# A two-layer Perceiver block: routing the first expert layer's tokens into slots of 48 per expert

## The reference

```python
E, K, H, F = (64, 6, 256, 96)
CAP = 2 * (T * K // E)                      # 48
...
buf = jnp.zeros((E, CAP + 1, H), x.dtype).at[se, slot].set(x[tok])[:, :CAP]
h = jax.nn.silu(jnp.einsum('ech,ehf->ecf', buf, w_gate)) * jnp.einsum('ech,ehf->ecf', buf, w_up)
out = jnp.einsum('ecf,efh->ech', h, w_down)
...
y = _routed_moe(x, topk_w, topk_ids, w_gate, w_up, w_down)
shared = jax.nn.silu(x @ ws_gate) * (x @ ws_up) @ ws_down
```

## Time and profile before

| | |
|---|---|
| median of three runs | 820.96 us (811.13 to 823.92) |
| profiled execution, its own time | 819.23 us |
| its span | 817.5 us |
| mean granted clock of TensorE | 0.884 of 2.4 GHz |
| first expert layer: first instruction, and first of the next stage | 195.06 and 346.29 us |
| TensorE busy, of the span | 680.8 us (83%) |
| VectorE, ScalarE, GpSimd busy | 534.1, 384.9, 314.9 us |

### The profile page before, as it was taken

One profiled execution on the slowest core, in us unless ns is written; L12 is line 12 of the kernel. 1 busy time (PEld: TensorE's weight loads), 2 busy tenths in 40 slices (PEclk: granted clock), 3 DMA queues, 4 the chain that ended last, 5 costly groups with the idle time before them and its releaser, 6 DMA issues. The chain is left out here.

```text
span 817.5 us, 12900 instructions
## 1 busy us (share of the span) xinstructions
PE 680.8 (83%) x4484; PEld 437.6 (54%) x4484; DVE 534.1 (65%) x771; ACT 384.9 (47%) x727; POOL 314.9 (39%) x233
## 2 busy tenths in 40 slices
PE   3735799987899999878998469888898778999997
PEld 1322345445577776556776225555555455666775
DVE  3379799993422222269999599999989963533221
ACT  2214555542122222234555378898989972303221
POOL 0064589891000000013444077787877871000000
PEclk9976999997999999988999666886868966999999
DMA  9637000003043433032443558586686742930000
GB/s 370 246 131 283 1 0 0 0 1 120 20 155 120 169 115 116 0 110 68 127 127 98 156 127 148 128 177 139 135 165 114 175 91 56 423 158 0 0 0 13
DMA packets 94718, 93.68 MB, mean 115 GB/s; under 512 B 69520, under 2 KB 87120, under 8 KB 88272
## 3 DMA queue, kind: packets, MB, share of 16 engines
q1 hardware_dynamic: 82128, 86.78, 36.5%
q10 hardware_dynamic: 12544, 6.29, 2.6%
HBM read 69.66 MB, written 6.62 MB: 93 GB/s over the span
## 5 line engine op out<-in xcount | busy, mean ns | idle before, releaser
L1489 DVE TENSOR_REDUCE d_nmax<-d_psum 128x1 f32<-128x1024 f32 x128 | 152.8, 1212 | 13.9 <-PE d_psum L1611 13.7
L1611 PE MATMUL d_psum<-d_kst,d_qT 96*128 96x512 bf16 x256 | 105.2, 515 | 36.9 <-DMA d_kst<-kT_scratch 23.4
L430 POOL TENSOR_TENSOR b_h<-b_h,b_cb 128x1024 f32<-128x1024 f32 x32 | 84.6, 2645 | 31.4 <-DVE b_h L484 30.9
L1465 POOL TENSOR_SCALAR d_rounded<-w_early,d_lift 128x1024 f16<-128x1024 f32 x64 | 71.8, 1122 | 29.5 <-ACT d_lift L1566 25.1
L1562 ACT ACTIVATE d_e<-d_psum,d_nmax 128x1024 f32<-128x1024 f32 x64 | 71.2, 1116 | 18.1 <-DVE d_nmax L1489 17.7
L484 DVE TENSOR_TENSOR_SCAN b_h<-b_dA,b_psum 128x1024 f32<-128x1024 f32 x32 | 73.0, 2285 | 7.6 <-PE b_psum L588 4.8
L1562 ACT ACTIVATE w_early<-d_psum,d_nmax 128x1024 f32<-128x1024 f32 x64 | 71.4, 1115 | 13.6 <-DVE d_nmax L1489 13.3
L544 ACT ACTIVATE b_dA<-b_dtT,b_A 128x248 f32<-128x248 f32 x128 | 53.7, 491 | 49.3 <-DVE b_h L484 43.4
L841 DVE TENSOR_TENSOR c_prod<-c_silu,c_psum 128x384 f32<-128x384 f32 x32 | 17.7, 554 | 90.1 <-ACT c_silu L884 90.1
L1465 POOL TENSOR_SCALAR d_rounded<-d_e,d_lift 128x1024 f16<-128x1024 f32 x64 | 72.8, 1137 | 9.6 <-ACT d_lift L1566 2.2
L1275 PE MATMUL k_psum<-k_wkv,k_ctxT 128*128 128x256 f32 x256 | 67.4, 395 | 5.4 <-issue 5.4
(11 more groups left out here) (375 smaller groups left out, 1285.3 us busy)
## 6 DMA issues: line engine op xcount, KB each, us to landing
d_kst<-kT_scratch SPq DMA_DIRECT2D x96, 128.0 KB, 2.7
w_early<-in_w SPq DMA_DIRECT2D x8, 1152.0 KB, 5.1
w_late<-in_w SPq DMA_DIRECT2D x8, 1152.0 KB, 5.1
w<-in_w SPq DMA_DIRECT2D x8, 1088.0 KB, 20.5
b_cb<-c_scratch SPq DMA_DIRECT2D x4, 2048.0 KB, 7.2
kT_scratch<-k_kT ACTq DMA_DIRECT2D x16, 384.0 KB, 2.8
a_ctxT<-in_ctxT SPq DMA_DIRECT2D x2, 2048.0 KB, 12.7
a_ctx<-in_ctx SPq DMA_DIRECT2D x2, 2048.0 KB, 21.2
```

Source lines behind the costliest of these rows:

```text
L430: nc.gpsimd.tensor_tensor(hv, hv, cv, ALU.mult).then_inc(hc_ready, 1)
L1465: nc.gpsimd.tensor_scalar(tile_of(r, j), e[j], lift[t][:, f:f + 1], HALF_ULP_ONE, ALU.mult, ALU.add).then_inc(r_ready, 1)
L1489: nc.vector.tensor_reduce(nm[:, t, m:m + 1, f:f + 1], quarter(m, j).unsqueeze(1), AX.X, ALU.max, negate=True).then_inc(nm_ready, 1)
L1611: last = nc.tensor.matmul(quarter(m, j)[:, b * 512:(b + 1) * 512], qT[0:QROWS, m:m + 1, t * P:(t + 1) * P], kst[m % 2][0:QROWS, at:at + 51 ...
```

## The change

The `MOE0` branches leave `moe_stage`, and a new `moe0_stage` takes its place in the list of stages. It gathers the tokens of four experts into 4 x 48 = 192 slots, computes gate, up and down for the slots only, and adds the results back to the tokens:

- `choose` (VectorE) builds the 0/1 matrix `pick` (128 tokens x 4 experts x 48 slots, bf16) for each half of the tokens by comparing the count `r.pos` with the slot number. A token that did not choose the expert has `FAR` added.
- `gather` (TensorE) multiplies `pick` by the normed input, which is split into three bf16 parts whose sum is the float32 value: 12 bf16 matmuls of 192 columns.
- `gate_up`: for each pair of experts and each half of the features, the two experts' gathered tokens stand in the array as 64 columns each (48 and 16 more that are not used), with results in PSUM partitions 0 to 63 and 64 to 127: 8 float32 matmuls of 192 columns.
- `turn` transposes two tiles of `a`; `turn_back` transposes four tiles of `pickw`, which GpSimd made from `pick` and the router's weights.
- `down`: 4 float32 matmuls of 256 columns, again with 64 columns standing. `add_back`: 4 float32 matmuls of 256 columns with `back` (128 columns) standing, accumulated in `acc[t]`.

In round `it`, TensorE gathers group `it`, does gate and up of `it - 1`, the transposes of `it - 2`, down of `it - 3` and the adding of `it - 4`. There are 16 + 4 rounds, written out. A group's weights come in two transfers, 768 and 384 KB. The accumulator bank is first cleared by a float32 matmul of zeros. The six more semaphores in `g["spent"]` are only cleared by GpSimd. ScalarE's remaining functions, `gate` and `keep_aT`, are a silu of 128x192 and a copy of 96x256 a round.

```diff
+GRP = 4
+NGRP = E0 // GRP
+PAIRS = GRP // 2
+SLOTS = GRP * CAP0
+HALF = P // 2
+GU0 = 2 * F0
+WGU0 = KC * GRP * GU0
+WDN0 = GRP * D
...
+def load_experts0(sp, g, d, grp, s):
+
+    sp.dma_start(g["w0"][s][:, 0:WGU0], d["w0gu"][grp]).then_inc(g["w0_in"][s], 16)
+    sp.dma_start(g["w0"][s][0:F0, WGU0:SLOT0], d["w0dn"][grp]).then_inc(g["w0_in"][s], 16)
...
+    nc.vector.tensor_tensor(r.selb[:, :, :], r.rep[:, :, 0:E0], r.ext[:, :, 0:E0], ALU.not_equal).then_inc(sem_sel, 1)
     step(nc.vector.tensor_tensor(r.sel[:, :, :], r.rep[:, :, 0:E0], r.ext[:, :, 0:E0], ALU.not_equal))
-    nc.vector.tensor_copy(r.selb[:, :, :], r.sel[:, :, :]).then_inc(sem_sel, 1)
+    step(nc.vector.tensor_scalar(r.pos[:, :, :], r.sel[:, :, :], -FAR, FAR, ALU.mult, ALU.add))
...
+                for grp in range(4, NGRP):
+                    sp.wait_ge(down_done, grp - 3)
+                    load_experts0(sp, g, d, grp, grp % 4)
...
+                for grp in range(NGRP):
+                    pool.wait_ge(pick_ready, grp + 1)
+                    if grp >= 2:
+                        pool.wait_ge(back_done, grp - 1)
+                    nc.gpsimd.tensor_tensor(pickw[grp % 2][:, :, :, 0:CAP0], pick[grp % 3][:, :, :, :],
+                                            r.w[:, :, grp * GRP:(grp + 1) * GRP].unsqueeze(3).to_broadcast([P, TC, GRP, CAP0]),
+                                            ALU.mult).then_inc(pickw_ready, 1)
...
+                dve.wait_ge(count_done, 1)
+                nc.vector.tensor_tensor(r.pos[:, :, :], r.pos[:, :, :], count_psum, ALU.add).then_inc(pos_ready, 1)
...
+                def choose(grp):
+                    if grp >= 3:
+                        dve.wait_ge(gather_done, grp - 2)
+                        dve.wait_ge(pickw_ready, grp - 2)
+                    for t in range(TC):
+                        last = nc.vector.tensor_tensor(
+                            pick[grp % 3][:, t, :, :], slot[:, :].unsqueeze(1).to_broadcast([P, GRP, CAP0]),
+                            r.pos[:, t, grp * GRP:(grp + 1) * GRP].unsqueeze(2).to_broadcast([P, GRP, CAP0]), ALU.is_equal)
+                    last.then_inc(pick_ready, 1)
+
+                def multiply(grp):
+                    dve.wait_ge(silu_ready, grp + 1)
+                    if grp >= 2:
+                        dve.wait_ge(aT_done, grp - 1)
+                    nc.vector.tensor_tensor(a[grp % 2][:, :, :], silu[grp % 2][:, :, :], gu_psum[:, :, F0:],
+                                            ALU.mult).then_inc(a_ready, 1)
+
+                def keep_back(grp):
+                    dve.wait_ge(back_done, grp + 1)
+                    if grp >= 3:
+                        dve.wait_ge(added, grp - 2)
+                    nc.vector.tensor_copy(back[grp % 3][:, :, :], st_psum).then_inc(back_ready, 1)
+
+                def keep_out(grp):
+                    dve.wait_ge(down_done, grp + 1)
+                    if grp >= 2:
+                        dve.wait_ge(added, grp - 1)
+                    nc.vector.tensor_copy(out[grp % 2][:, :, :], out_psum).then_inc(out_ready, 1)
+
+                choose(0)
+                choose(1)
+                for it in range(NGRP + 4):
+                    if it + 2 < NGRP:
+                        choose(it + 2)
+                    if 1 <= it <= NGRP:
+                        multiply(it - 1)
+                    if 2 <= it <= NGRP + 1:
+                        keep_back(it - 2)
+                    if 3 <= it <= NGRP + 2:
+                        keep_out(it - 3)
+                dve.wait_ge(added, NGRP)
+                step(nc.vector.tensor_tensor(x[:, :, :], x[:, :, :], ps[:, ACC, :].rearrange("p (t c) -> p t c", t=TC), ALU.add))
...
+                act.wait_ge(xnT_done, 1)
+                nc.scalar.activation(xnT[:, :, :], ps[:, OUT, :].rearrange("p (k t) -> p k t", k=KC),
+                                     ACT.Copy).then_inc(xnT_ready, 1)
+                act.wait_ge(xn_ready, 1)
+                nc.scalar.activation(xp[0][:, :, :], xn[:, :, :], ACT.Copy).then_inc(part_ready, 1)
...
+                def keep_gathered(grp):
+                    act.wait_ge(gather_done, grp + 1)
+                    if grp >= 2:
+                        act.wait_ge(gu_done, grp - 1)
+                    nc.scalar.activation(xT[grp % 2][:, :, 0:SLOTS], xt_psum, ACT.Copy).then_inc(xT_ready, 1)
+
+                def gate(grp):
+                    act.wait_ge(gu_done, grp + 1)
+                    if grp >= 2:
+                        act.wait_ge(a_ready, grp - 1)
+                    nc.scalar.activation(silu[grp % 2][:, :, :], gu_psum[:, :, 0:F0], ACT.Silu).then_inc(silu_ready, 1)
...
+                nc.tensor.matmul(ps[:, ACC, :].rearrange("p (a b) -> p a b", a=4), g["zeros"][:, :],
+                                 g["zeros"][:, :].unsqueeze(1).to_broadcast([P, 4, P]), start=True, stop=False,
+                                 skip_group_check=True)
...
+                def gather(grp):
+                    pe.wait_ge(pick_ready, grp + 1)
+                    if grp >= 1:
+                        pe.wait_ge(xT_ready, grp)
+                    for k in range(KC):
+                        for t in range(TC):
+                            for q in range(3):
+                                last = nc.tensor.matmul(xt_psum[:, k, :], xp[q][:, t, k * P:(k + 1) * P],
+                                                        pick[grp % 3][:, t, :, :].rearrange("p e s -> p (e s)"),
+                                                        start=(t == 0 and q == 0), stop=(t == TC - 1 and q == 2))
+                    last.then_inc(gather_done, 1)
+
+                def gate_up(grp):
+                    pe.wait_ge(g["w0_in"][grp % 4], 32 * (grp // 4 + 1))
+                    pe.wait_ge(xT_ready, grp + 1)
+                    if grp >= 1:
+                        pe.wait_ge(a_ready, grp)
+                    w = g["w0"][grp % 4][:, 0:WGU0].rearrange("p (k e f) -> p k e f", k=KC, e=GRP)
+                    for q in range(PAIRS):
+                        for k in range(KC):
+                            for h in range(2):
+                                e = 2 * q + h
+                                last = nc.tensor.matmul(gu_psum[h * HALF:(h + 1) * HALF, q, :],
+                                                        xT[grp % 2][:, k, e * CAP0:e * CAP0 + HALF], w[:, k, e, :],
+                                                        start=(k == 0), stop=(k == KC - 1), skip_group_check=True)
+                    last.then_inc(gu_done, 1)
+
+                def turn(grp):
+                    pe.wait_ge(a_ready, grp + 1)
+                    if grp >= 1:
+                        pe.wait_ge(aT_ready, grp)
+                    else:
+                        pe.wait_ge(shared_aT_ready, 1)
+                    for q in range(PAIRS):
+                        last = nc.tensor.transpose(at_psum[:, q, :], a[grp % 2][:, q, :], ident[:, :])
+                    last.then_inc(aT_done, 1)
+
+                def turn_back(grp):
+                    pe.wait_ge(pickw_ready, grp + 1)
+                    if grp >= 1:
+                        pe.wait_ge(back_ready, grp)
+                    for q in range(PAIRS):
+                        for t in range(TC):
+                            last = nc.tensor.transpose(st_psum[:, q, t * P:(t + 1) * P],
+                                                       pickw[grp % 2][:, t, 2 * q:2 * q + 2, :].rearrange("p e s -> p (e s)"),
+                                                       ident[:, :])
+                    last.then_inc(back_done, 1)
+
+                def down(grp):
+                    pe.wait_ge(aT_ready, grp + 1)
+                    if grp >= 1:
+                        pe.wait_ge(out_ready, grp)
+                    w = g["w0"][grp % 4][0:F0, WGU0:SLOT0].rearrange("p (e c) -> p e c", e=GRP)
+                    for q in range(PAIRS):
+                        for h in range(2):
+                            last = nc.tensor.matmul(out_psum[h * HALF:(h + 1) * HALF, q, :],
+                                                    aT[grp % 2][:, q, h * HALF:(h + 1) * HALF], w[:, 2 * q + h, :],
+                                                    start=True, stop=True, skip_group_check=True)
+                    last.then_inc(down_done, 1)
+
+                def add_back(grp):
+                    pe.wait_ge(back_ready, grp + 1)
+                    pe.wait_ge(out_ready, grp + 1)
+                    for q in range(PAIRS):
+                        for t in range(TC):
+                            last = nc.tensor.matmul(acc[t], back[grp % 3][:, q, t * P:(t + 1) * P], out[grp % 2][:, q, :],
+                                                    start=False, stop=(grp == NGRP - 1 and q == PAIRS - 1),
+                                                    skip_group_check=True)
+                    last.then_inc(added, 1)
+
+                for it in range(NGRP + 4):
+                    if it < NGRP:
```

(15 more changed lines are left out.)

335 lines of the change are left out of this document (232 added, 103 removed).

## The result

The changed kernel takes 782.85 us (median of four runs: 780.54, 780.86, 784.83, 789.67); the kernel before, measured beside it, took 816.17 (four runs, 811.13 to 823.92). The ratio is 0.967, with a 95% interval of 0.962 to 0.972. It is not the quotient of the two medians, since it leaves out runs more than 1.5% above the fastest of their kernel. The forecast was 784, in a range of 776 to 815.

A forecast was written before the change was run, and what follows sets the result against it. TensorE's streaming was taken to bound the expert stage: start 212.6 + 16 rounds x 5.9 + 1.9 + 0.6 = 309.5, next stage at 310.9 against 346.49. So 819.2 - 35.6 = 784 us, range 776 to 815.

The forecast's parts named there:

- The bound: Expert stage: bound by TensorE's streaming, so a change is worth a sum over its matmuls; new round 5.9 us against 8.40.
- The other engines' work a round: Each round of the new stage: VectorE 2.5 us, ScalarE some 1.2, GpSimd 0.9, all under TensorE's 5.9.
- the margin of the weights: Weight transfers of a group: landing takes 5.1 us, read some 8.8 us later; holds down to rounds of about 3.5 us.
- 64 standing at half price: Gate, up and down: about half the 128-standing price, two experts side by side in different output partitions; 784 us, chance 0.70.
- The price of a record: Gate and up: 0.095 us for each of 16 records of 192 columns, with an allowance for weight loads; 1.5 us a round.
- Rival B: Gate, up and down: 64 standing costs as much as 128; rounds of 7.75 us, kernel 813 us, chance 0.14.
- The changes of width: Four switches between 64 and 128 columns standing in each round: 0.15 us for all four.
- rival C: Every change of width waits for the array to run empty: 0.34 us by 64 changes, kernel 803 us, chance 0.05.
- The beginning: Stage start: gather begins at 212.6 against 212.01; lower clock costs 1.9 us, the second gather's wait 0.6.
- The end: Last rounds run down without waits; last matmul ends at 309.5, next stage starts 1.4 us later, at 310.9 against 346.49.
- Rivals D and E: D: stage at 1.2 GHz throughout, kernel 878, chance 0.07. E: hand-over, transfer or fetching paces rounds, 802, chance 0.04.
- everything behind the barrier stays: Stages after the expert stage: move forward unchanged, so the whole 35.6 us saving comes off the profiled 819.2.

The follow-up runs named there:

- the repeat: The changed kernel run once more without an edit: profiled 792.56 us, expert stage 122.0 us, median of six runs 784.97, ratio 0.969 to the kernel before.
- the two repeats: The kernel before and the changed kernel, each profiled once more without an edit: 821.11 and 792.56 us, expert stages 149.8 and 122.0 us.
- the last run: The changed kernel once more, unedited, measured beside three others: median of six runs 784.97 us, ratio 0.969 to the kernel before.

## Why the prediction held, and where it did not

**The bound was right.** The stage is a sum of TensorE's streaming: busy without gaps in every window from 221 us on, and less or more work moved the stage by about 16 times what it moved the round (128 standing 25.3 for 25.0, one bf16 part 9.8 for 10.6). The other engines' work a round came out as forecast: by the window from 240 to 256 us 2.5 us on VectorE, 1.2 on ScalarE and 1.0 on GpSimd. What was too generous is the margin of the weights, said to hold down to rounds of 3.5 us: a single wait of 0.2 to 0.4 us for them shows up at rounds of 5.5 and 5.8.

**64 standing at half price was right, its picture was not.** I leaned on experts beside each other in different halves. Neighbours in the same half cost nearly the same (0.06 us a round more); what runs together is the pair of records that starts at once. The price of a record was too high: 0.095 with an allowance for loads, where a pair takes 0.163, 0.081 each. The 0.097 for 32 standing and 256 columns was misread too: the 31 records include those that reach over the window's edges. By their starts (the first at 28.08, the last at 30.98) two go every 0.22 us, 0.11 each, about half. Rival B is refuted by the round of 7.73 that it costs when it is really built. At half price the change gains 1.56 us a round more than at full price, 25 us of the stage.

**The changes of width were the mis-sized term.** I took 0.15 for all four, since the row of 32 columns showed a start 0.07 ahead of a modelled end. A modelled end says nothing of a hole. By starts that one change costs little as well: the last four records there begin at 19.95, and the transposes follow at 20.75, after 0.80 us,

```profile
19.95 0.87 PE L282 MATMUL a_psum<-a_ctxT,a_xnT 128*32 128x512 f32 x4
```

where such a set lasts 0.85 (see the last section). The step that failed was to carry this single row, from 32 columns to 128, over to changes between 64 and 96 or 128; why it is cheaper stays open. Two changes fewer are worth 0.35. With 0.16 each the parts add up in every round: 0.98 + 1.30 + 0.66 + 0.87 + 1.72 = 5.53 without any; four changes make 6.17 (measured 6.17), two 5.85 (5.82), and with 128 standing, which has none, 1.30 and 0.87 double and 7.70 stands against 7.73. So a loss at each change is there, as rival C had it, at half of the 0.34 that it was priced at. The Trainium skill, page TensorEngine Tiling, section Key Properties, says that a change of tiling mode drains TensorE. The 0.16 us of each change agree with that, though no row shows the drain itself. The two errors, 0.22 too much for the matmuls (nearly all of it gate and up, 1.5 against 1.30) and 0.49 too little for the changes, leave 0.27 a round, 4.3 us of the stage.

**The beginning.** Gather began 17.3 us into the stage (forecast 17.5), the second waited 0.73 (0.6), and the lower clock cost 2.2 (1.9), 3.8 in the repeat. **The end.** The next stage began 1.2 after the last matmul (1.4). The stage's sum by the measured terms is 17.3 + 16 x 6.17 + 2.2 + 0.7 + 1.2 = 120.1; the trace has 120.4. Against the forecast of -35.6 the stage gave -30.8, and between the two repeats -27.8.

**Rivals D and E** left no sign in the changed kernel: clock 1.00 behind 221 us, no wait of TensorE inside a round.

**The total was helped by another stage, and that was luck.** The sum started from a profile in which the key and value stage ran in its long rhythm, and assumed that everything behind the barrier stays. The profile of the changed kernel has the short one, which gave 9.6 us that nobody forecast and hides the 4.8 that the expert stage fell short. Had it been the long one, the profiled time would have been some 790 (the repeat took 792.56), 6 to 9 us above the forecast and still in its range. Like against like the change is worth 27 to 29 us (819.2 and 821.11 against 792.56) in the long rhythm, and some 30 (811 against 781) where both are short, if the kernel before is short at 811: that was not seen in a profile of it, only in its times. Medians, which mix both, differ by 33.3 here and by 26.8 beside the last run. What decides which rhythm an execution falls into stays open; so does the rest of the scatter, in the first stages and the second attention.

## What to carry to other kernels

Price a matmul by its columns times its passes, and look at what stands: a float32 matmul with 64 columns or fewer standing cost half here, in whatever half it lies, but each change between 64 and 96 or 128 took it partly back, so narrow work belongs together. Moving such work within a round also moves the hand-overs, and the last rounds, where less stands between maker and reader, are where a new wait appears. Before a total is forecast, take several profiles of the kernel before: a stage that the change does not touch can have two lengths, two profiles can show the same one (they did here), and 10 us of 800 can be luck.

## What the runs showed of the hardware that I had not expected

- With 64 columns standing, float32 records start in twos, about 0.01 us apart in the changed kernel, and two take 0.163 us for 192 columns, 0.215 for 256; with 128 standing each takes that alone. Where 32 stand, four start together in the first stage, and the timelines there that end at 17.5 and at 18.5 show a set of four of 512 columns lasting 1.96 - 1.11 = 0.85 us, 0.21 for each:

```profile
17.39 1.11 PE L282 MATMUL a_psum<-a_ctxT,a_xnT 128*32 128x512 f32 x4 [1.20 <-DMA a_ctxT<-in_ctxT]
17.39 1.96 PE L282 MATMUL a_psum<-a_ctxT,a_xnT 128*32 128x512 f32 x8 [1.20 <-DMA a_ctxT<-in_ctxT]
```

- A change between 128 or 96 and 64 columns standing costs 0.16 to 0.17 us; one between 128 and 96 costs nothing.
- A loop over three engines has two rhythms, 4.65 and 5.25 us a step, by which of two instructions comes first. An execution settles into one within four of its 16 steps and keeps it; one wait holds it in the short one, in both profiles taken with it.
